# A decoder layer's feed-forward as Strassen products: two token tiles against halves of K and pairs of column blocks, in two passes

## The reference

```python
x = _layernorm(x + _L0_attn_ref(x))                          # autocorrelation "attention"
x = _layernorm(x + _L0_xattn_ref(ctx_4096, ctx_4096, x))     # cross-attention
out = xf @ W_base.T + _moe_lora(xf, gate_W, A, B)            # W_base 2048 x 2048
x = _layernorm(x + out)

def _moe_lora(xf, gate_W, A, B):
    gate_probs = softmax(xf @ gate_W.T)                      # 8 experts
    weights, sel = top_k(gate_probs, 2); weights /= sum(weights)
    h = einsum('td,erd->ter', xf, A)                         # rank 8
    h = h * (w_dense[:, :, None] * 2.0)
    return einsum('ter,eor->to', h, B)
```

## Time and profile before

| | |
|---|---|
| median of 3 runs | 2077.42 us (2074.51 to 2078.51) |
| the profiled execution | 2076.62 us |
| its span | 2074.7 us |
| TensorE busy | 1955.9 us, 94% |
| VectorE, ScalarE, GpSimd busy | 41%, 29%, 15% |
| mean granted TensorE clock | 0.991 |
| feed-forward | from about 600 us to the end |

### The profile page before, as it was taken

One profiled execution on the slowest core, in us unless ns is written; L12 is line 12 of the kernel. 1 busy time (PEld: TensorE's weight loads), 2 busy tenths in 40 slices (PEclk: granted clock), 3 DMA queues, 4 the chain that ended last, 5 costly groups with the idle time before them and its releaser, 6 DMA issues.

```text
span 2074.7 us, 28253 instructions
## 1 busy us (share of the span) xinstructions
PE 1955.9 (94%) x11264; PEld 1048.8 (51%) x11264; DVE 855.5 (41%) x2167; ACT 606.8 (29%) x771; POOL 317.1 (15%) x529
## 2 busy tenths in 40 slices
PE   3998989898957999999999999999999999999998
PEld 2666666666633444444444444444444444444443
DVE  4777777777757332222232222232222223222221
ACT  5777777777646110000010000011000011000000
POOL 2344444444315000000000000000000000000000
PEclk9999999999979999999999999999999999999999
DMA  8899999999667222111232211123111122221121
GB/s 264 219 291 260 286 261 290 260 294 267 212 216 244 82 92 71 61 61 61 63 102 77 61 61 61 61 91 91 61 61 61 61 80 92 71 61 61 61 61 41
DMA packets 288910, 271.17 MB, mean 131 GB/s; under 512 B 261504, under 2 KB 261632, under 8 KB 265984
## 3 DMA queue, kind: packets, MB, share of 16 engines
q1 hardware_dynamic: 288832, 270.17, 43.7%
HBM read 138.02 MB, written 67.11 MB: 99 GB/s over the span
## 4 chain that ended last, share of the span: by engine, by line
PE 67%; ACT 1%; DVE 1%; DMA 1%; POOL 1%; issue 0%; ACTq 0%; POOLq 0%
PE ps_y_f L1117 62%; PE ps_a_f L1136 2%; PE ps_y_f L1121 1%; PE ps_y_f L1122 1%; PE ps_a_f L1137 1%; ACT w_hi_f L912 1%; DMA cbuf<-w_chunks 0%; DVE w_lo_f L986 0%; DMA chunk<-w_chunks 0%; POOL w_lo_f L895 0%; POOL cbuf L894 0%; PE ps_h_f L1144 0%; DVE b_stack_f L1072 0%; ACT y_f L973 0%; PE ps_t_f L1102 0%
## 5 line engine op out<-in xcount | busy, mean ns | idle before, releaser
L1117 PE MATMUL ps_y_f<-w_hi_f,x_hi_f 128*128 128x512 f16 x2048 | 777.8, 380 | 10.9 <-POOL w_lo_f L895 8.1
L1117 PE MATMUL ps_y_f<-w_hi_f,x_lo_f 128*128 128x512 f16 x2048 | 777.9, 380 | 0.0
L1117 PE MATMUL ps_y_f<-w_lo_f,x_hi_f 128*128 128x512 f16 x2048 | 777.7, 380 | 0.0
L973 ACT ACTIVATE y_f<-y_f,nb_f,rs_f 128x2048 f32<-128x2048 f32 x32 | 67.0, 2094 | 1112.3 <-POOL nb_f L903 1112.3
L1117 PEld LDWEIGHTS ps_y_f<-w_hi_f,x_hi_f 128*128 128x128 f16 x2048 | 200.6, 98 | 248.5 <-POOL w_lo_f L895 10.6
L1117 PEld LDWEIGHTS ps_y_f<-w_hi_f,x_lo_f 128*128 128x128 f16 x2048 | 200.7, 98 | 242.6 <-issue 1.7
L1117 PEld LDWEIGHTS ps_y_f<-w_lo_f,x_hi_f 128*128 128x128 f16 x2048 | 200.7, 98 | 233.7 <-issue 1.4
L997 DVE SCALAR_TENSOR_TENSOR y_f<-ps_y_f,w_iscale,xn_f 128x512 f32<-128x512 f32 x64 | 46.6, 748 | 476.6 <-PE ps_y_f L1122 476.6
L997 DVE SCALAR_TENSOR_TENSOR y_f<-ps_y_f,w_iscale,xn 128x512 f32<-128x512 f32 x64 | 46.5, 748 | 448.5 <-PE ps_y_f L1122 448.5
L900 POOL TENSOR_TENSOR var_eps_f<-mv_f,columns 128x1 f32<-128x1 f32 x32 | 6.0, 189 | 1357.0 <-DVE mv_f L1085 1357.0
L654 PE MATMUL ps_s_fast<-k_both_fast,q_hi_fast 128*128 128x256 f16 x1024 | 169.9, 274 | 0.0
(11 more groups left out here) (160 smaller groups left out, 2083.9 us busy)
## 6 DMA issues: line engine op xcount, KB each, us to landing
xbuf_fast<-x SPq DMA_DIRECT2D x32, 1024.0 KB, 7.8
x_scratch<-x2buf_fast SPq DMA_DIRECT2D x32, 1024.0 KB, 6.3
out<-y_f SPq DMA_DIRECT2D x32, 1024.0 KB, 4.0
cbuf<-ctx_in SPq DMA_DIRECT2D x16, 1024.0 KB, 5.7
cbuf_fast<-ctx_in SPq DMA_DIRECT2D x16, 1024.0 KB, 6.8
xn<-w_chunks SPq DMA_DIRECT2D x16, 1024.0 KB, 7.7
xn<-x_scratch SPq DMA_DIRECT2D x16, 1024.0 KB, 4.7
xn_f<-x_scratch SPq DMA_DIRECT2D x16, 1024.0 KB, 4.8
```

The costliest lines, as they stand in the source:

```text
L973: nc.scalar.activation(y[parity][:], y[parity][:], ACT.Identity, bias=nb_[:, 0:1], scale=rs[:, 0:1]).then_inc(out_ready, 1)
L1117: nc.tensor.matmul(ps_y[j][:], xx[parity][:, k], ww[:, k, j * BANK:(j + 1) * BANK], start=(k == 0 and xx is x_hi and ww is w_hi), stop=False)
```

## The change

The feed-forward works on pairs of tiles. For a pair, the rows x are a 2 x 2 matrix A of blocks (tile 0 or 1, first or second half of K), the weights for 1024 output columns a 2 x 2 matrix of blocks (half of K, 512 columns). Their product's four blocks C11, C12, C21, C22 (tile, column block) come from seven block products instead of eight. Each product has one of seven sums of A's blocks (`A_ITEM`) on one side, one of seven sums of weight blocks on the other, and all sums are split into float16 halves; a product is 8 K tiles x 3 matmuls of 512 columns into a bank of its own.

- The seven weight sums need 7/4 of the room of the weights themselves, so only 1024 output columns are held: the kernel goes over all 16 pairs for the first 1024 columns, then backwards over them for the second. A step for one pair and one pass is called a slot: s = 0 to 15 first pass, 16 to 31 second. Slot 16 has the pair of slot 15 and uses its items again. The residual result of the first pass (`y_scratch`), the LoRA operand h (`h_scratch`) and the statistics (`saved`) are kept for the second; the router runs in the first pass alone.
- The weights come in "units", one K tile of each half of K by 1024 columns (1 MB). For each unit GpSimd makes two sums and VectorE two differences (`unit_sums`, `unit_low`), ScalarE the high halves, VectorE the low halves. Eight units are made ahead of and during slot 0 and eight more during slot 15, where TensorE goes K tile by K tile over all seven products, and each K tile of weights is overwritten when it has passed.
- The items: of the seven sums of rows, two are rows themselves. The other five are made by GpSimd in one buffer, `sums` (`combine`). ScalarE makes the high half, VectorE the low half (`low_rows`) into one of two buffers, and one transposing DMA turns both (`turn`). The items of slot s + 1 are made during slot s.
- A product goes into up to two of the four result blocks. VectorE adds it there (`update`, 14 per slot, in the order of `UPDATES`), on float32 rows in SBUF; the first update of a block takes the rows x as its other operand. The next pair's x may be loaded after update 3 (`next_x`).
- LoRA blocks L12 and L21 reuse banks 4 and 5, and TensorE waits for updates 5 and 7 before them; L22 and L11 are added into banks 2 and 3 after their products.
- In the second pass each slot ends with the statistics of both passes' columns, GpSimd's four small steps (`norm`), four ScalarE passes (`normalise`) and two stores (`store_out`); the first pass's half is loaded in between (`load_first`).
- The preload at the end of the attention is the first unit instead of three chunks, and the two first tiles aren't turned by TensorE any more. The loops are written out for all 32 slots.

The core of the diff. The first `for s in range(SLOTS)` is SP's, the second VectorE's.

```diff
--- before.py
+++ after.py
...
-                    def main(j):
...
-                            for xx, ww in ((x_hi, w_hi), (x_hi, w_lo), (x_lo, w_hi)):
-                                nc.tensor.matmul(ps_y[j][:], xx[parity][:, k], ww[:, k, j * BANK:(j + 1) * BANK],
-                                                 start=(k == 0 and xx is x_hi and ww is w_hi), stop=False)
...
-                    def low_rows():
-                        if nxt and not turned_on_pe(t + 1):
-                            dve.wait_ge(hi_done, rows_split(t + 1))
-                            v.tensor_tensor(rows_lo, xn[1 - parity][:], rows_hi, ALU.subtract).then_inc(t_free, 1)
...
+    NP_ = PAIRS_OF_TILES
+    SLOTS = 2 * NP_
+    HK = KT // 2
+    A_ITEM = ["A11", "A22", "A21-A11", "A12-A22", "A11+A22", "A21+A22", "A11+A12"]
+    assert len(A_ITEM) == NM
+    UPDATES = [(0, C12, 1), (0, C22, 1), (1, C11, 1), (1, C21, 1), (4, C11, 1), (4, C22, 1), (5, C21, 1), (5, C22, -1),
+               (6, C11, -1), (6, C12, 1), ("L12", C12, 1), ("L21", C21, 1), (2, C22, 1), (3, C11, 1)]
...
+        SOURCES = [(half(0, 0), None), (half(1, 1), None), (half(1, 0), half(0, 0)), (half(0, 1), half(1, 1)),
+                   (half(0, 0), half(1, 1)), (half(1, 0), half(1, 1)), (half(0, 0), half(0, 1))]
+        SIGN = [None, None, ALU.subtract, ALU.subtract, ALU.add, ALU.add, ALU.add]
...
+                def next_x(s):
+                    if makes(s):
+                        sp.wait_ge(a_sum, 5 * made(s))
+                        sp.wait_ge(added, NU * (s - 1) + 4)
+                        for t in range(2):
+                            load_x(s, t)
...
+                def turn(s, i):
+                    if makes(s):
+                        g = item(s, i)
+                        sp.wait_ge(a_lo, g + 1)
+                        if s:
+                            sp.wait_ge(pe_done, NE * (s - 1) + i + 1)
+                        sp.dma_start_transpose(a_cols[:, i], rows[g % 2][:].rearrange("p a c -> p (a c)")).then_inc(a_turned[g % 2], 16)
...
+                def store_first(s):
+                    sp.wait_ge(added, NU * (s + 1))
+                    sp.dma_start(y_scratch[token(s)], y[s % 2][:]).then_inc(y_stored[s % 2], 16)
...
+                def store_out(s):
+                    sp.wait_ge(normalised, 2 * (s - NP_) + 1)
+                    sp.dma_start(rows_out(s, 0), y_first).then_inc(first_stored, 16)
+                    sp.wait_ge(normalised, 2 * (s - NP_) + 2)
+                    sp.dma_start(rows_out(s, 1), y[s % 2][:]).then_inc(y_stored[s % 2], 16)
...
+                for s in range(SLOTS):
+                    if s and s <= NP_:
...
+                        load_b(1)
+                    if s > NP_:
+                        store_out(s - 1)
+                        load_h(s)
+                    if s == LAST_OF_FIRST:
+                        sp.wait_ge(b_split, 1)
+                        load_unit(HK)
+                        sp.wait_ge(y_stored[0], 16 * (NP_ // 2))
+                        for u in range(HK + 1, 2 * HK):
+                            load_unit(u)
+                    turn(s + 1, 0)
+                    turn(s + 1, 1)
+                    if s >= NP_:
+                        load_first(s)
+                    for i in range(2, NM):
+                        turn(s + 1, i)
+                store_out(SLOTS - 1)
+                for i in range(2):
...
+                def combine(s, i):
+                    if makes(s):
+                            wait_x(pool, s, t)
+                            pool.wait_ge(w_lo_done, 4 * 2 * HK)
+                        g.tensor_tensor(sums[:], SOURCES[i][0], SOURCES[i][1], SIGN[i]).then_inc(a_sum, 1)
...
+                def unit_sums(u):
+                    raw, both = stage[stage_of(u)], pair_sum[u // HK]
+                    wait_unit_loaded(pool, u)
+                        pool.wait_ge(a_lo, NM * NP_)
+                    g.tensor_tensor(both, raw[:, 0::2], raw[:, 1::2], ALU.add).then_inc(w_sum, 1)
+                    pool.wait_ge(w_lo_done, 4 * u + 1)
+                    pool.wait_ge(w_sum, 4 * u + 3)
+                    g.tensor_tensor(raw[:, 0], raw[:, 0], raw[:, 3], ALU.add).then_inc(w_sum, 1)
...
+                        else:
+                            act.wait_ge(a_sum, 5 * made(s) + i - 1)
+                            source = sums[:]
+                        after(act, a_turned[gi % 2], 16 * (gi // 2))
+                        nc.scalar.activation(rows[gi % 2][:, 0], source, ACT.Copy).then_inc(a_hi, 1)
...
+                def normalise(s):
+                    act.wait_ge(ln_ready, s - NP_ + 1)
+                    act.wait_ge(first_loaded, 16 * (s - NP_ + 1))
+                    for data in (y_first, y[s % 2][:]):
+                        nc.scalar.activation(data[:, 0], data[:, 0], ACT.Identity, bias=nb_[:, 0:1], scale=rs[:, 0:1])
+                        nc.scalar.activation(data[:, 1], data[:, 1], ACT.Identity, bias=nb_[:, 1:2], scale=rs[:, 1:2]).then_inc(normalised, 1)
...
+                        dve.wait_ge(a_hi, gi + 1)
+                        source = SOURCES[i][0] if i < 2 else sums[:]
+                        v.tensor_tensor(rows[gi % 2][:, 1], source, rows[gi % 2][:, 0], ALU.subtract).then_inc(a_lo, 1)
...
+                def unit_low(u):
+                    raw, kk = stage[stage_of(u)], u % HK
+                    def low(part, source, n):
+                        dve.wait_ge(w_hi_done, 4 * u + n)
+                        v.scalar_tensor_tensor(w_lo[:, part, kk], source, w_scale[:], w_hi[:, part, kk], ALU.mult,
+                                               ALU.subtract).then_inc(w_lo_done, 1)
+                    low(slice(5, 7), raw[:, 0::3], 1)
+                    dve.wait_ge(w_sum, 4 * u + 1)
+                    v.tensor_tensor(raw[:, 1], raw[:, 1], raw[:, 3], ALU.subtract).then_inc(w_sum, 1)
+                    v.tensor_tensor(raw[:, 2], raw[:, 2], raw[:, 0], ALU.subtract).then_inc(w_sum, 1)
+                    low(slice(2, 4), pair_sum[u // HK], 2)
+                    low(slice(0, 2), raw[:, 1:3], 3)
+                    low(4, raw[:, 0], 4)
...
+                def update(s, u):
+                    source, (t, j), sign = UPDATES[u]
+                    at = slice(j * BANK, (j + 1) * BANK)
...
+                        base = x_rows[t][:, ps * HL + j * BANK:ps * HL + (j + 1) * BANK]
+                    dve.wait_ge(pe_done, NE * s + update_event(u))
+                    v.scalar_tensor_tensor(acc, bank[bank_of_update[u]][:], (w_iscale if sign > 0 else minus_iscale)[:], base, ALU.mult,
...
+                for s in range(SLOTS):
+                    if s == LAST_OF_FIRST:
+                        router_scores(s)
+                        router_weights(s)
+                        for u in range(HK, 2 * HK - 2):
+                            unit_low(u)
+                    for u in range(4):
+                        update(s, u)
+                    low_rows(s + 1, 0)
+                    low_rows(s + 1, 1)
+                    if s < LAST_OF_FIRST:
+                        router_scores(s)
+                    low_rows(s + 1, 2)
+                    if s < LAST_OF_FIRST:
+                        router_weights(s)
+                    low_rows(s + 1, 3)
+                    update(s, 4)
+                    update(s, 5)
+                    low_rows(s + 1, 4)
+                    update(s, 6)
+                    update(s, 7)
+                    low_rows(s + 1, 5)
+                    update(s, 8)
+                    update(s, 9)
+                    finish(s)
+                    if s == LAST_OF_FIRST:
+                        unit_low(2 * HK - 2)
+                        unit_low(2 * HK - 1)
+                        b_low(1)
+                    low_rows(s + 1, 6)
+            @block.tensor
...
+                def step(i, kk):
+                    for part, ww in ((0, w_hi), (0, w_lo), (HK, w_hi)):
+                        ins = nc.tensor.matmul(bank[i][:], a_cols[:, i, part + kk, :], ww[:, i, kk, :],
+                                               start=(kk == 0 and part == 0 and ww is w_hi), stop=(kk == HK - 1 and part == HK and i not in (2, 3)))
+                    return ins
...
+                    own = name in ("L12", "L21")
+                    if own:
+                        pe.wait_ge(added, NU * s + read_of(LORA_BANK[name], name))
+                    nc.tensor.matmul(target[:], h_t[:, t, 0], b_stack[:, 0, at], start=own, stop=False)
+                    nc.tensor.matmul(target[:], h_t[:, t, 1], b_stack[:, 1, at], start=False, stop=True).then_inc(pe_done, 1)
```

766 lines of the change are left out of this document (412 added, 354 removed).

## The result

The changed kernel takes 2239.71 us (median of 4 runs, 2235.65 to 2244.39) against 2075.97 for the kernel before beside it: ratio 1.079, 95% interval 1.078 to 1.081. The forecast was 2180 with a range of 2090 to 2250: slower, as expected, 60 us further than forecast, and 10 us inside the upper bound. The profiled execution took 2238.1 us, 1.8 more than its span.

The account below looks back on a forecast made before the run. TensorE, busy 94%, bounds the kernel before. Start 739, first-pass slots 640, turn 130, second-pass slots 616, last slot 38 and tail 15 make 2178, with 1.9 beyond the span 2180 us; range 2090 to 2250.

Parts of the forecast that it names:

- the gain of 157 us: Feed-forward on TensorE: 336 matmuls per pair instead of 384, 79.8 us against 89.6, over sixteen pairs.
- the chains beside TensorE: Feed-forward slots: serial work on other engines and DMA makes slots 45.7 and 44.0 us against TensorE's 41.85 and 38.0.
- x landed 8.4: First pass: the next pair's two x tiles land 8.4 us after update 3, between 7.5 and about 1.9 later.
- The exclusion: GpSimd sums and two-input VectorE operations block each other: item 1's low half waits out a sum, router's add costs 1.7 us.
- TensorE waits 3 us for update 7 in the first pass: Before LoRA block L21: update 7 stands behind low half 4, so TensorE, ready 27 us after update 3, waits 3 us.
- "I take half" of the clock's loss, 0.8 us: First-pass slot: a wait may halve TensorE's clock, losing about 1.7 us; half was taken, giving 45.7 us.
- the row at 672: Feed-forward start, old kernel: an idle stretch there kept clock 1.00; a similar one around 624 was followed by 0.50.
- The loop of the second pass, 44.0: From one slot's aggregated statistics through norm, stores, x and items to the next: 44 us against TensorE's 38.0.
- The start: Weight units of 9.1 us, 12.7 with an item, make slot 1 begin at 739, 63 us later; bounds 721 to 750.
- The turn: Between passes, weight units remade: slots 15 and 16 take 130 us where TensorE needs 80; bounds 118 and 138.
- Rival B: Both passes: the DMA queue is the bound, slots about 47.5 us, 2260 in all; chance 0.13.
- Rival A: Both passes: feeding hides and TensorE sets slots of 41.85 and 38.0 us, 2037 in all; chance 0.10.

Follow-up runs that it names:

- experiment 6: Changed kernel with orders alone altered: updates 6 to 9 and copy of h earlier, stores behind transposes, second-pass x first; 2080.01 us, 1.0034 of the kernel before.
- Experiments 4 and 10: 4: changed kernel with first-pass store behind the first two transposes, 2219.11 us; 10: changed kernel with updates 6 to 9 and copy of h earlier, 2195.06 us.
- experiment 5: Changed kernel with the five item sums of each pair made on VectorE instead of GpSimd; 2202.90 us, 1.0613 of the kernel before.
- experiment 2: Changed kernel with VectorE doing updates 6 and 7 before the low half of item 4, 8 and 9 before that of item 5; 2201.14 us.
- experiment 8: Changed kernel with the orders of experiment 6 and all sums (items, weights, start) on VectorE; 2054.11 us, 0.9903 of the kernel before.
- experiment 11: Experiment 6 without the second pass's load of first halves (1 MB per slot), so results are wrong; 2077.41 us, 1.0014 of the kernel before.
- experiment 1: Changed kernel with the next pair's x loads issued ahead of the two stores in the second pass; 2231.09 us, 1.0755 of the kernel before.
- experiment 9: Changed kernel with only SP's queue order from experiment 6, VectorE and ScalarE orders unchanged; 2134.93 us, 1.0288 of the kernel before.
- experiment 12: Experiment 8 with h loaded right behind x in the second pass and the start's item sums ahead of their weight units; 2043.60 us, 0.9862.

## Why the prediction was right, and where it was 60 us short

- **TensorE's work and the gain of 157 us**: right. 5376 matmuls, and 41.3 and 38.4 us per slot once nothing disturbs them (experiment 6).
- **Slower, because the chains beside TensorE are longer than its slot**: right. Orders alone give 160 us back.
- **x landed 8.4**: 8.6 in the mean. Experiments 4 and 10 confirm that the store ahead of it is in the term (7.5 us with the store moved behind, 10.7 where it is issued closest ahead).
- **The exclusion**: the blocked low half (2.45) and the router's add (1.77 over its 0.16, where 1.7 was taken) were there. But taking these 3 us of record away, with five sums more on VectorE, was worth 1 us of slot (experiment 5), and 0.1 to 0.3 with the orders right.
- **TensorE waits 3 us for update 7 in the first pass**: it waits 3.6, but for two things: 1.4 for update 7 and 2.1 for the copy of h. The prediction had given that copy 0.6 us as if ScalarE were free; it stands behind the high half of item 4, as update 7 does. When one wait went, the other took half of it over (experiment 2). So the total was right and its parts were not.
- **"I take half" of the clock's loss, 0.8 us**: this was mis-sized. TensorE worked 42.8 us per first-pass slot against 41.25: 1.6, nearly the whole of the 1.7, for which the prediction had shown no row. What the row at 672 did, waits with the clock kept at 1.00, came in 5 slots of 14. That is the 11 us of the first pass. Of the second pass's 40.4 us, 2.0 go in experiment 6 with the waits, but there TensorE was not what set the slot.
- **The loop of the second pass, 44.0**: mechanism right, term short by 2.5, 35 us of the 60. In the mean x's second tile was there 18.0 us after the statistics, not 15.3, and the next aggregation came 28.5 after that, where 28.6 was predicted. So the shortfall lies wholly between the statistics and x, in three pieces. The norm took 2.3 instead of 1.35, because its first step (1.05 in the turn shown above, 0.20 in the last slot) stands behind VectorE's low half of item 6: exclusion again, at a place where it had not been looked for. The issues cost 0.4 more (h's load between the stores and x was left out). And x landed 9.9 us after its issue, not 8.6, over the upper end of the 7.5 to 9.7 that had been allowed. GpSimd's first step in the last slot, with no low half beside it:

```profile
2225.50 0.20 POOL L1008 TENSOR_TENSOR var_eps_f<-mv_f,columns 128x2 f32<-128x2 f32 x1 [34.69 <-DVE mv_f L1247]
```

- **The start**: units took 8.55 and 11.85 (9.1 and 12.7 predicted), but GpSimd's first sum began only at 617.2, 5.6 us after VectorE made the same one in experiment 8 (611.6). That nearly cancels, by luck: the units end at 702.7 (701.4). The rest of the 5 us is behind them, where TensorE waits 4.8 us for the copy of h.

```profile
617.19 2.33 POOL L998 TENSOR_TENSOR b_stack_f<-cbuf 128x1024 f32<-128x1024 f32 x1 [11.58 <-issue]
```

- **The turn**: six units 52.1 us as predicted (52.2); ahead of the first stood 5.6 us of waiting for its 1 MB, which SP had issued behind the store of y. That is the 5 us.
- **Rival B (the DMA queue, 47.5 in both passes, 2260)** came nearest in time, and for the wrong reason: the share was 0.62 and 0.75, experiment 6 runs with 0.90, and 1 MB per slot less gave 0.4 us there (experiment 11). Its true part is order: in all traces of this case the DMAs of SP's queue land in the order of their issue, so a transpose comes after all copies issued ahead of it.
- **Rival A (42 and 38)**: experiment 6 made it (42.5 and 39.9). But what the prediction had it depend on, x issued under 2 us after the statistics, was not it: x goes out 4.9 us after them in experiment 1 and 4.4 in experiment 6 (means), and the slots differ by 6.0. The stores had to go between the transposes.

Left open: why x lands late in three slots of experiment 9, what holds the second pass at 39.3 in experiment 12, why GpSimd's first sum is late, and how much of the gain in the weight units is exclusion.

## What to carry to other kernels

When a change makes the critical engine's work shorter, list what each in-order queue puts ahead of the next thing that engine needs, the copy queue first: here the same operations in another order were worth 160 us, and no single reordering more than 40, except the one that dealt with all copies. Waits in series can hide each other, so an experiment that removes one and gains little has not shown that it was harmless. Records that two engines lengthen for each other cost little where the chain has slack (0.1 to 0.3 us per slot here); where the two work in turn without slack, as in the weight units, moving all to one engine gave 1.2 to 1.4 us per unit.

## What the runs showed of the hardware that was not expected

- A transpose that takes 3.8 us alone was not done 10 us after its issue with 2 MB of x, two stores of 1 MB and a small load issued in the 7 us before it (experiment 1). In all 14 traces of this case (340 to 576 DMAs of SP's queue each) none landed before one issued ahead of it.
- A GpSimd sum of two SBUF rows holds up a VectorE cast of 128x4 with one SBUF input (1.86 us in place of 0.16) but not maxima, index searches or a reduction (0.15 to 0.17).
- TensorE's two waits of 0.9 and 1.5 us at 970 are followed by LoRA matmuls of 0.61 to 0.63 us instead of 0.38 to 0.39, a granted clock of 0.50; at 786 waits of 0.8 and 1.5 us are not, and the matmuls stay at 0.38. With experiment 6's waits of 0.7 to 1.8 us per slot the first pass stays at 1.00.
- The exclusion works in both directions on small operations: GpSimd's 128x2 add of the norm takes 1.05 us beside a VectorE low half, 0.20 without one.
